# Four-layer conditioned stack on one core: the attention mask is added on GpSimd instead of by a product on TensorE

## What is computed

```python
scores = jnp.einsum('bhqd,bhkd->bhqk', q / math.sqrt(HEAD_DIM), k)
scores = scores + attention_bias                                    # (32, 16, 256, 256)
scores = jnp.where(src_mask, -jnp.inf, scores.astype(jnp.float32))  # mask (32, 1, 256, 256)
probs = jax.nn.softmax(scores, axis=-1).astype(v.dtype)
```

## Time and profile before

| | |
|---|---|
| median of 3 runs | 2158.73 us (2158.18 to 2162.78) |
| the profiled execution | 2160.82 us |
| its span, first to last instruction | 2159.0 us |
| mean granted TensorE clock | 0.975 |

### The profile page before, as it was taken

One profiled execution on the slowest core, in us unless ns is written; L12 is line 12 of the kernel. 1 busy time (PEld: TensorE's weight loads), 2 busy tenths in 40 slices (PEclk: granted clock), 3 DMA queues, 4 the chain that ended last, 5 costly groups with the idle time before them and its releaser, 6 DMA issues.

```text
span 2159.0 us, 43618 instructions
## 1 busy us (share of the span) xinstructions
PE 1946.9 (90%) x14354; PEld 1688.8 (78%) x14354; DVE 1610.5 (75%) x5373; ACT 1363.3 (63%) x2179; POOL 293.6 (14%) x393
## 2 busy tenths in 40 slices
PE   5678999999999999999999999999999999999876
PEld 4567888888888888888788787888888887888665
DVE  4357778888777788877777887777888877777753
ACT  3246667676666776677677666666676676677332
POOL 1111101111110111111111111111111111111100
PEclk8689999999999999999999999999999999999888
DMA  6364556555455566554556555556555555654430
GB/s 217 111 185 147 160 156 195 182 191 183 152 166 149 176 193 188 167 174 130 184 178 187 178 160 177 150 186 197 181 188 182 168 150 155 193 179 137 134 104 10
DMA packets 222312, 356.13 MB, mean 165 GB/s; under 512 B 29523, under 2 KB 120147, under 8 KB 222068
## 3 DMA queue, kind: packets, MB, share of 16 engines
q1 hardware_dynamic: 222068, 352.99, 52.6%
HBM read 294.12 MB, written 58.79 MB: 163 GB/s over the span
## 4 chain that ended last, share of the span: by engine, by line
PE 69%; DVE 19%; issue 6%; ACT 3%; DMA 1%; SPq 0%; POOL 0%; ACTq 0%; DVEq 0%; POOLq 0%
PE pD L441 45%; PE pX L656 11%; PE pS L441 9%; DVE bias_ring L1142 8%; DVE bias_ring L939 6%; PE pC L441 2%; PE pC L678 1%; DVE x_nat L936 1%; DVE crossed L936 1%; ACT gelu_out L746 1%; ACT L746 1%; DMA branch_row<-in_branch_rows 1%; ACT probs L746 1%; ACT hid L746 0%; DVE ctx_nat L936 0%
## 5 line engine op out<-in xcount | busy, mean ns | idle before, releaser
L1142 DVE CUSTOM_DVE_ANT_0 bias_ring<-pS,bias_ring 128x256 f32<-128x256 f32 x1024 | 389.7, 418 | 226.9 <-PE pS L441 225.1
L746 ACT ACTIVATE probs<-pX 128x512 f32<-128x512 f32 x512 | 304.4, 595 | 235.7 <-PE pX L656 233.8
L746 ACT ACT_TABLE_LOAD x342 | 438.8, 1283 | 22.3 <-PE pD L441 15.6
L656 PE MATMUL pX<-ident,bias_ring 128*128 128x128 f32 x2048 | 325.4, 282 | 115.9 <-DVE bias_ring L939 97.3
L656 PEld LDWEIGHTS pX<-ident,bias_ring 128*128 128x128 f32 x2048 | 227.8, 141 | 218.5 <-DVE bias_ring L939 209.9
L939 DVE TENSOR_SCALAR bias_ring<-bias_ring,row_max 128x256 f32<-128x256 f32 x1024 | 338.4, 373 | 18.3
L441 PE MATMUL pS<-k_stack,q_stack 96*128 96x256 f32 x1024 | 304.7, 380 | 0.0
L441 PE MATMUL pD<-x,raw 128*128 128x256 f32 x1024 | 251.4, 389 | 5.1 <-ACT gelu_out L746 2.6
L441 PE MATMUL pD<-raw,gelu_out 128*128 128x256 f32 x1024 | 237.6, 380 | 2.8 <-DVE y_nat L936 2.8
L441 PEld LDWEIGHTS pD<-x,raw 128*128 128x128 f32 x1024 | 191.4, 194 | 31.2 <-issue 7.5
L441 PEld LDWEIGHTS pS<-k_stack,q_stack 96*128 96x128 f32 x1024 | 197.9, 193 | 20.1 <-issue 0.2
(11 more groups left out here) (148 smaller groups left out, 3679.4 us busy)
## 6 DMA issues: line engine op xcount, KB each, us to landing
bias_ring<-in_fside SPq DMA_DIRECT2D x512, 256.0 KB, 3.3
raw<-in_experts SPq DMA_DIRECT2D x128, 512.0 KB, 4.6
q_spill<-hid SPq DMA_DIRECT2D x96, 256.0 KB, 3.5
k_spill<-hid SPq DMA_DIRECT2D x96, 256.0 KB, 3.4
q_stack<-q_spill SPq DMA_DIRECT2D x128, 192.0 KB, 3.5
k_stack<-k_spill SPq DMA_DIRECT2D x64, 384.0 KB, 4.8
norm<-in_expert_rows SPq DMA_DIRECT2D x32, 384.0 KB, 4.0
x_nat<-in_x SPq DMA_DIRECT2D x32, 256.0 KB, 3.1
```

Of the source, the lines that this page charges most:

```text
L656: last = e.transpose(pX[:, k, t * P:(t + 1) * P], bias_ring[:, u % NBIAS, t, k * P:(k + 1) * P], ident[:, :])
L746: return e.activation(o, i, func, bias=bias, scale=scale)
L1142: e.tensor_tensor_reduce(bias_ring[:, n, t, :], pS[:, t, :], bias_ring[:, n, t, :], 1.0, -3.4e38, ALU.add, ALU.max, row_max[:, n, t:t + 1] ...
```

## The change

The product with the mask is dropped on PE, and GpSimd adds the mask to the head's bias in its slot of the ring, between the bias's landing and the maxima. The mask is now one f32 buffer, so ACT's cast waits until all 16 adds of the sequence before are done. DVE waits for `masked` in place of the DMA. All five strings and their skips are new; GpSimd's now has the 16 letters h.

```diff
 ORDER = {
-    "PE": "hhfhhfhhhhfrrhhfrhhfhhhghhhghhrhhghhhhhhgrgrhhgghhrgghhrfhhhhfrrhhfr",
-    "ACT": "rhrhrfhrrhfrrrhfrhfrfhhfhrfrhfhhrhghhghhhgrhghg",
-    "DVE": "hrhfrhrfhrhfhhrfhrfhghrhhhrhhfhfrhrhrfhrfghrfg",
-    "POOL": "ffrgrfgf",
-    "SP": "hfhfhhfhhhhffggrhhhhhhghghg",
+    "PE": "frhhfrhhhrhhhrrhhfrhhffhhhghhhghhrhhghhhhhhggrhhgrgfhhgghhfrhhhhfrhh",
+    "ACT": "hfhfrhrhfrrhrfrhrhrhrhrfrfrhfhrfhhghghhhghhgrhg",
+    "DVE": "hrhrrhhrfhrfhfghrhhhrhhfhhffrhfrhfrghfrhhfrhgr",
+    "POOL": "hhhfhhhhhfhfhgfhrhhrghhh",
+    "SP": "fhhhhhffgrhhhhhghgghhfhfhhg",
 }
-SKIP = {"PE": (9, 101, 37), "ACT": (13, 56, 55), "DVE": (12, 53, 47), "POOL": (4, 0, 6), "SP": (10, 42, 4)}
+SKIP = {"PE": (9, 101, 40), "ACT": (13, 56, 55), "DVE": (10, 50, 46), "POOL": (5, 37, 6), "SP": (8, 39, 4)}
...
-        eye_bf = sb("eye_bf", [P, P], BF16)
...
-        mask_add = sb("mask_add", [P, 2, T, S], BF16)
+        mask_add = sb("mask_add", [P, T, S])
...
                 def scores(h):
                     g, par, u = h // 2, h % 2, u0 + h
-                    if not u:
-                        e.wait_ge(sem["dve_eye"], 1)
-                    e.wait_ge(sem["mask_made"], b + 1)
                     e.wait_ge(sem[f"dma_stack{2 * g // NPAIR}"], 48 * (b + 1))
                     if u:
                         e.wait_ge(sem["max_made"], 2 * u)
-                    mm(pS[:, :, :], eye_bf[:, :], mask_add[:, b % 2, :, :], True, False)
                     for t in range(T):
-                        last = mm(pS[:, t, :], q_stack[:, g, par, t * P:(t + 1) * P], k_stack[:, g, :], False, True)
+                        last = mm(pS[:, t, :], q_stack[:, g, par, t * P:(t + 1) * P], k_stack[:, g, :], t == 0, t == T - 1)
...
-                if b >= 2:
-                    e.wait_ge(sem["scored"], 16 * (b - 1))
-                act(flat(mask_add[:, b % 2, :, :]), flat(mask_u8[:, :, :]), ACT.Copy, scale=MASKED).then_inc(sem["mask_made"], 1)
+                if b:
+                    e.wait_ge(sem["masked"], NH * b)
+                act(flat(mask_add[:, :, :]), flat(mask_u8[:, :, :]), ACT.Copy, scale=MASKED).then_inc(sem["mask_made"], 1)
...
                 def maxima(u):
                     n = u % NBIAS
                     e.wait_ge(sem["scored"], u + 1)
-                    e.wait_ge(sem[f"dma_bias{n}"], 16 * (u // NBIAS + 1))
+                    e.wait_ge(sem["masked"], u + 1)
...
             def attention(b):
-                return
-                yield
+                for u in range(NH * b, NH * b + NH if b < NB else 0):
+                    n = u % NBIAS
+                    e.wait_ge(sem["mask_made"], b + 1)
+                    e.wait_ge(sem[f"dma_bias{n}"], 16 * (u // NBIAS + 1))
+                    e.tensor_tensor(flat(bias_ring[:, n, :, :]), flat(bias_ring[:, n, :, :]), flat(mask_add[:, :, :]),
+                                    ALU.add).then_inc(sem["masked"], 1)
+                    yield
```

More of the change, by code:

```diff
@@ L52 @@
     "dve_set", "dve_angles", "act_sine", "act_emb", "dve_rot", "dve_cols",
-    "pe_mod", "dve_mod", "pe_folded", "dve_folded", "dve_zeros", "dve_eye", "pool_set", "pool_ident",
+    "pe_mod", "dve_mod", "pe_folded", "dve_folded", "dve_zeros", "pool_set", "pool_ident",
     "dma_w0", "dma_w1", "dma_w2", "dma_w3", "dma_w4", "act_w", "dve_w",
@@ L61 @@
     "dve_deep", "branch_done", "x2_made", "x2_biased", "x2_turned", "x2_hi", "x2_lo", "qkv", "qk_hi", "qk_lo",
-    "v_made", "mask_made",
+    "v_made", "mask_made", "masked",
     "scored", "max_made", "subtracted", "turned", "exp_made", "valued", "ctx_copied", "ctx_turned", "rden_made", "ctx_made",
@@ L945, in vector_program @@
             e.memset(pC[:, :, :], 0.0).then_inc(sem["dve_zeros"], 1)
-            e.wait_ge(sem["pool_ident"], 2)
-            e.tensor_copy(eye_bf[:, :], ident[:, :]).then_inc(sem["dve_eye"], 1)
             e.wait_ge(sem["dma_ints"], 16)
```

## The result

The changed kernel takes 2342.12 us (median of 4 runs, 2331.39 to 2351.64) against 2160.71 for the kernel before beside it (4 runs): a ratio of 1.0839, 95% interval 1.0789 to 1.0888. It is 181 us slower, where 2140 was forecast and 2208 was the end of the range. The profiled execution took 2331.39 us, so its rows belong to the fastest of the four runs.

The account below looks back on a forecast made before the run. PE was taken as the bound, with DVE close behind. Product -93, stretching +61, equal stretch +40 and strings -27 summed to -19 us; with 2.1 more off the profiled 2160.8 that gave 2140 us, range 2062 to 2208.

Parts of the forecast that it names:

- The product, -93: On PE, dropping the mask's product saves 0.22 us for each of about 422 heads on the chain: -93 us.
- GpSimd isn't the bound, and no addition is late: On GpSimd, 512 additions of 1.28 us bring it to about 950 us, 44% of the span, each ending before its maxima.
- The price of an addition, 0.38 us: On DVE, each GpSimd addition stretches instructions by 0.38 us, 195 us in all, priced from the 128 additions of before.
- My upper end, 0.87: On DVE, the highest stretching per addition, 0.87 us, from the excess of a pair on L1041 beside GpSimd's additions.
- The share on the chain, 31%: Of DVE's 195 us of stretching, 31% reaches the chain, midway between 25% and 38%: +61 us.
- the two are then equal: Per sequence, DVE rises from 51.0 to 57.1 us and PE falls from 60.6 to 57.1.
- The stretch of equal engines, +40: From 1023 to 1039, where DVE has 0.53 us left, four additions cost 1.24 us more per sequence: +40 us.
- ACT's mask: nothing: ACT's cast waits for the 16th addition of the sequence before, which comes just in time: no cost.
- The strings, -27: Five new engine orders, a quarter of the best case of removing PE's 109 us of idle time: -27 us.
- DVE becomes the bound: Rival: port blocking on DVE at 0.66 us per addition, 38% on the chain, gives 2207 us; chance 0.28.
- What would show it: Signs in the profile: PE's busy time down about 196 us, L939's mean about 450 to 470 ns, DVE over 25% of chain.
- the signs of the wrong kind: DVE waiting for bias_ring from GpSimd before maxima, ACT waiting for GpSimd before mask_add, or DVE's waits for GpSimd's roots.

Follow-up runs that it names:

- the pair with and without pacing: New strings, nine heads' mask added on GpSimd, seven by PE's product: 2133.37 us with additions waiting for the subtraction three heads before, 2266.9 us without that wait.
- memsets: Changed kernel with each GpSimd addition replaced by two 128x512 memsets that only write, mask not applied: 2160.71 us, ratio 1.0001 to the kernel before.
- halves: Changed kernel with each GpSimd addition cut into two of 128x256: 2292.51 us, ratio 1.0603 to the kernel before.
- paced: Changed kernel with each addition also waiting until the head three before is subtracted, and two bf16 mask buffers: 2211.09 us, ratio 1.0222 to the kernel before.
- the work aside: Changed kernel with GpSimd's 512 instructions working on the mask's own buffer, DVE waiting only for the bias's landing, mask not applied: 2260.87 us, ratio 1.0464.

## Why the prediction was wrong

In measured steps: 2160.7 before; the new strings -12 (2149.5); the product -58 (2091.7); the additions +250; sum 2341. The forecast missed by 202 us: 149 of them are the additions (61 + 40 forecast, 250 measured), 35 the product, 15 the strings.

- *The product, -93.* Wrong in size: 48 us with the old strings, 58 with the new. I took the heads that stand on the chain times 0.22; PE's busy time fell by 0.17 per head. The chain names the longest way, not by how much it is longer than the next; with DVE at 27% and ACT at 9% of it after the edit, half the saving was gone.
- *GpSimd isn't the bound, and no addition is late.* Right: 961.4 us busy (950 forecast), 1.34 us each, no wait of DVE for one.
- *The price of an addition, 0.38 us.* Wrong in size: 0.55. It was the mean over four additions per sequence, two of which meet hardly anything: before, those to x_nat held DVE up by 0.9 us each and those of branch_row by 0.7, the two to res by under 0.1. With 20 per sequence, in bursts where several biases land together, both subtractions of a pair can wait for one each. I had also counted two forms of DVE's instructions only; the second scaling of the expert's norm, the gate and the rotation stretched too. My upper end, 0.87, held it.
- *The share on the chain, 31%.* This is the step that failed. It measured 0.9 in the changed kernel (0.85 by the profiled executions), and 0.98 in the pair with and without pacing; the others gave 0.7 (memsets), 0.8 (halves, paced) and 1.0 (the work aside), never near 0.31. With my price and this share, 512 x 0.38 x 0.9, the additions would have come to 175 us; with the measured price and my share, to 87. I had written that both engines would then need 57.1 us per sequence, "the two are then equal", and still weighed DVE's delays with its share while PE had 69%. The likely reason, which no run isolates: in a ring of PE and DVE with one pS between them, a delay that no reserve takes up goes to the end whole.
- *The stretch of equal engines, +40.* Right in kind (DVE full at 15.76 of 16 us, PE not), but it wasn't one stretch that paid: DVE has 42% of the whole chain, in place of 19%.
- *ACT's mask: nothing.* Right; the mask isn't waited for in the profile beyond the start (4.2 us on GpSimd), and ACT waits for the additions before its cast 1.0 us in all. *The strings, -27*: -12, between its ends.
- *The rival "DVE becomes the bound"* had the right mechanism, and its threshold of 0.50 us per addition was passed. Its price of 0.66 was near the 0.55 measured; its share of 38% kept it at 2207. With the measured figures in it, 0.55 x 512 x 0.9 = 253 and -58 - 12, its sum gives 2344; as these come from the result, that is no test of it.
- *What would show it:* PE's busy time fell by 40 us, not 196. I had added up the single times of the products, which overlap: taking the product out alone lowers it by 88 us (old strings) or 81 (new), and the rest came back with the additions (see below on the clock). The subtractions' mean rose to 532, over the 470 forecast, and the price of 0.55 is beyond the 0.5 that I had named as wrong in size; DVE's share of the chain is 42%, over 25% as forecast. Of the signs of the wrong kind there are traces only: ACT's 1.0 us, and 3 us for the roots.

## What to carry to other kernels

Before work is moved to GpSimd, list DVE's instructions that take two SBUF operands or a tensor and a scalar from SBUF: here each could wait for a whole instruction of GpSimd (a write held up only the second sort), and in the burst shown every one did. If it must be moved, cut it short and tie its start to a moment behind which DVE is known to do other things; a wait that paces it (here `subtracted` of three heads before) was worth 134 us. Look at what stands behind the paced instruction on its own engine, as that is held up too. And when two engines come out equal in a sum, price further delays of either at most of their length (0.7 to 1.0 here), not by its share of the old chain.

## Not expected of the hardware

- *Alternation.* GpSimd's additions step in between two DVE instructions that follow each other at once (2.69 us for the pair, in the timeline above; 76 pairs of 512 with both subtractions over 0.6 us).
- *PE's clock.* Changed kernel, three stretches of 6 us (PE's busy time comes first, the granted clock is the third number from the end):

```profile
1072.00:1078.00 6.00, 5.56 (x47) 5.35 (x47) 4.03 (x9) 5.39 (x10) 2.46 (x2) 1.00 0.49 135
1078.00:1084.00 6.00, 3.07 (x24) 2.87 (x23) 2.44 (x5) 4.03 (x5) 1.53 (x2) 0.95 0.01 1
1084.00:1090.00 6.00, 6.00 (x41) 3.94 (x39) 4.28 (x17) 3.35 (x5) 0.00 (x0) 0.76 0.30 87
```

PE was idle for half of 1078 to 1084, and then part of its work ran at 1.2 in place of 2.4 GHz: a mean of 0.76 in the next stretch. Over the run the mean is 0.953, against 0.975 before, and the same 13842 products took 1907.4 us of busy time, where they took 1863.3 (at a mean of 0.966) in the run without product and additions. Some of what the additions cost can thus be paid on PE, as a slower clock after a wait. How much of the 250 us that is, no run sets apart, but there is an upper end: span times what the clock lacks of 1 is 2329.6 x 0.047 = 109 us with the additions and 2093.3 x 0.034 = 71 without, so as an estimate at most 38. The 44 us of busy time aren't all clock: a wait also ends the overlap between products. At the full clock, the four transposes of a turn take 0.60 us behind other products and 0.66 behind a wait (from 1006.47 and 1010.95).
